# The output tensor as accumulator: b3 and the output tiles of both output layers added by accumulating DMAs

## The reference

```python
xn = layernorm(x)                     # x: 8192 x 2048
a  = (xn @ W_in[:4096].T) @ conv_w.T  # 8192 x 4096
z  = silu(xn @ W_in[4096:].T)
g  = a * D * z
h1 = relu(xn @ W1.T + b1)             # 8192 x 4096
h2 = relu(h1 @ W2.T + b2)
out = x + g @ W_out.T + h2 @ W3.T + b3   # 8192 x 2048
```

## Time and profile before

| | us |
|---|---|
| median of three runs | 1817.83 (1816.61 to 2179.19) |
| the profiled execution | 1814.43 |
| its span on the slowest core (0) | 1812.9 |
| spans of the eight cores | 1805.3 to 1812.9 |
| PE busy | 1764.7 (97%) |
| DVE busy | 900.0 (50%) |
| ACT busy | 229.6 (13%) |
| POOL busy | 243.4 (13%) |
| DMA moved | 296.34 MB, mean 163 GB/s |

### The profile page before, as it was taken

One profiled execution on the slowest core, in us unless ns is written; L12 is line 12 of the kernel. 1 busy time (PEld: TensorE's weight loads), 2 busy tenths in 40 slices (PEclk: granted clock), 3 DMA queues, 4 the chain that ended last, 5 costly groups with the idle time before them and its releaser, 6 DMA issues.

```text
span 1812.9 us, 24809 instructions; the slowest of 8 cores (1805.3 to 1812.9 us)
## 1 busy us (share of the span) xinstructions
PE 1764.7 (97%) x9984; PEld 978.1 (54%) x9984; DVE 900.0 (50%) x1130; ACT 229.6 (13%) x355; POOL 243.4 (13%) x270
## 2 busy tenths in 40 slices
PE   2999999999999999999999999999999999999998
PEld 2444444444444444444444444444444888888887
DVE  6744444444444585444444753333334754466443
ACT  4111122222222200000000011111111000000000
POOL 6222230000000000000000000000000122222221
PEclk9899999999999999999999999999999999999999
DMA  9576764444438543334444822333336765885532
GB/s 290 153 217 216 229 209 124 124 137 140 126 121 276 158 150 117 122 122 133 140 140 155 286 86 96 109 116 116 117 116 207 247 197 175 263 272 186 163 117 71
DMA packets 58016, 296.34 MB, mean 163 GB/s; under 512 B 7600, under 2 KB 7600, under 8 KB 40368
## 3 DMA queue, kind: packets, MB, share of 16 engines
q1 hardware_dynamic: 29376, 167.79, 31.4%
q0 software_dynamic: 28240, 126.89, 19.8%
q10 hardware_dynamic: 288, 0.08, 0.0%
HBM read 227.62 MB, written 67.11 MB: 163 GB/s over the span
## 4 chain that ended last, share of the span: by engine, by line
PE 93%; DMA 3%; DVE 2%; issue 1%; ACT 1%; POOL 0%; DVEq 0%; SPq 0%; ACTq 0%; POOLq 0%
PE ps L293 73%; PE ps L850 19%; DMA sF<-H1S 1%; DMA PS<-sM 1%; DMA sM<-XB 1%; DVE sF L240 1%; DVE sW L240 1%; DMA sF<-X 1%; DVE sST L313 1%; ACT sF L390 0%; PE ps L369 0%; ACT sM L352 0%; DVE sM L335 0%; DVE sM L912 0%; ACT sST L322 0%
## 5 line engine op out<-in xcount | busy, mean ns | idle before, releaser
L293 PE MATMUL ps<-sF,sW 128*128 128x512 bf16 (+1 forms) x6272 | 1357.3, 379 | 4.0 <-DVE sW L240 2.1
L293 PEld LDWEIGHTS ps<-sF,sW 128*128 128x128 f16 x6272 | 613.7, 98 | 746.2 <-issue 9.1
L240 DVE TENSOR_TENSOR sW<-sW 128x1024 f16<-128x1024 f16 (+1 forms) x480 | 446.1, 960 | 168.1 <-DMA sW<-W 127.1
L850 PE MATMUL ps<-sW,sF 128*128 128x256 f16 x3584 | 393.7, 273 | 3.5 <-DVE sW L240 2.0
L850 PEld LDWEIGHTS ps<-sW,sF 128*128 128x128 bf16 x3584 | 351.2, 98 | 46.0 <-issue 4.4
L542 DVE TENSOR_TENSOR sM<-ps,sM 128x512 f32<-128x512 f32 x80 | 55.3, 691 | 331.1 <-ACT sM L537 331.1
L598 DVE TENSOR_TENSOR sM<-ps,sM 128x512 f32<-128x512 f32 (+1 forms) x160 | 109.8, 687 | 119.6 <-PE ps L293 119.6
L537 ACT ACTIVATE sM<-ps 128x512 f32<-128x512 f32 x80 | 47.8, 597 | 606.1 <-PE ps L293 606.1
L240 DVE TENSOR_TENSOR sF<-sF 128x2048 bf16<-128x2048 bf16 (+2 forms) x92 | 101.9, 1169 | 2.9 <-DMA sF<-H1S 2.0
L579 ACT ACTIVATE sM<-sM,sCN 128x512 bf16<-128x512 f32 x64 | 46.0, 721 | 242.3 <-DVE sM L598 242.3
L547 DVE TENSOR_TENSOR sM<-ps,sM 128x512 f32<-128x512 f32 x80 | 54.8, 685 | 22.6 <-PE ps L293 22.6
(11 more groups left out here) (39 smaller groups left out, 347.6 us busy)
## 6 DMA issues: line engine op xcount, KB each, us to landing
sW<-W SPq DMA_DIRECT2D x48, 1024.0 KB, 8.7
sW<-WC SPq DMA_DIRECT2D x32, 1024.0 KB, 7.5
sW<-WX SPq DMA_DIRECT2D x32, 512.0 KB, 6.9
sW<-WZ SPq DMA_DIRECT2D x32, 512.0 KB, 6.6
sW<-W SPq DMA_DIRECT2D x32, 512.0 KB, 6.5
sW<-WO SPq DMA_DIRECT2D x16, 1024.0 KB, 7.9
X1S<-sM POOLq DMA_DIRECT2D x16, 512.0 KB, 7.4
sF<-X POOLq DMA_DIRECT2D x8, 1024.0 KB, 9.8
```

Of the source, the lines that this page charges most:

```text
L240: return line.do(lambda e: e.tensor_tensor(out, a, b, ALU.subtract if sub else ALU.add), c)
L293: return e.matmul(ps[bank][:], sW[:, c0 + k * 128:c0 + (k + 1) * 128], rhs[:, k * TH:(k + 1) * TH], start=st0, stop=last, skip_group_check ...
L850: return e.matmul(ps[bank][:, lo:lo + CW], lhs[:, k * TH + tp * 128:k * TH + (tp + 1) * 128], w[:, k * CW:(k + 1) * CW], start=start, stop ...
```

## The change

- XB and PS are gone. `x_copy(j)` copies 128 rows of X to OUT, from DRAM to DRAM, at the place of `xb_load(j)`; `b3_add(j)`, at the place of `xb_add(j)`, adds BB3 to these rows of OUT by an accumulating DMA, after the copy landed. POOL computes nothing there.
- `r_load` is gone. `o_close` writes the bare result to the ring: for products 3 and 4 a copy on ACT, for 6 and 7 one addition on DVE (bank plus E).
- `r_store(n)` adds the ring's tile to OUT by an accumulating DMA, in both output layers. An item of the second layer waits for the store of the same tile in the first (`n - 32`).
- The ring has 8 buffers, one per item of a chunk; `ring_free` waits for the store of item n - 8, on ACT or DVE, ahead of the close. The first eight wait for the last three stores of H2S.

```diff
+NRING = 8
...
 TM = [
-    dict(w="WO", src="GS", res="XB", dst="PS"),
-    dict(w="W3", src="H2S", res="PS", dst="OUT"),
+    dict(w="WO", src="GS"),
+    dict(w="W3", src="H2S"),
 ]
...
         def ring(i):
-            return sM[:, 2048 + i * 512:2048 + (i + 1) * 512]
+            return sM[:, 1024 + i * 512:1024 + (i + 1) * 512]
...
-        def xb_load(j):
...
-        def xb_add(j):
...
+        def x_copy(j):
+            rows = slice(j * 128, (j + 1) * 128)
+            tk_bs[("l", j)] = pool.do(lambda e: e.dma_start(dram["OUT"][rows, :], dram["X"][rows, :]),
+                                      c_bx[j % 2], 16)
+
+        def b3_add(j):
+            rows = slice(j * 128, (j + 1) * 128)
+            pool.need(tk_bs[("l", j)])
+            tk_bs[j] = pool.do(lambda e: e.dma_start(dram["OUT"][rows, :], dram["BB3"][:], accum_op=ALU.add,
+                                                        max_dma_last_dim=4096),
+                               c_bs[j % 2], 16)
...
-                bg = [tk_bs[6], tk_bs[7], tk_ba.get(7)]
+                bg = [tk_norm[j] for j in range(6)]
...
             if g < 16 and g % 2 == 1:
-                xb_load(g // 2)
+                x_copy(g // 2)
             if 1 < g <= 16 and g % 2 == 0:
-                xb_add(g // 2 - 1)
+                b3_add(g // 2 - 1)
...
-        def r_load(n):
...
         def r_store(n):
+
             si, c, m, u = items[n]
-            i = n % 6
-            pool.need(tk_ro[n])
-            dst = place(TM[si]["dst"], si, c, m, u)
-            tk_rst[n] = pool.do(lambda e: e.dma_start(dst, ring(i).rearrange("p (b i) -> p b i", b=2)), c_rs[i], 16)
+            i = n % NRING
+            pool.need(tk_ro[n], tk_rst.get(n - 32))
+            if n == 0:
+                pool.need(tk_bs[6], tk_bs[7])
+            dst = place("OUT", si, c, m, u)
+            tk_rst[n] = pool.do(lambda e: e.dma_start(dst, ring(i).rearrange("p (b i) -> p b i", b=2),
+                                                      accum_op=ALU.add), c_rs[i], 16)
...
+        def ring_free(line, n):
+
+            if n < NRING:
+                line.need(*e_start, *[tk_store[x] for x in (L, L - 1, L - 2)])
+            else:
+                line.need(tk_rst[n - NRING])
+
         def o_close(n):
             si, c, m, u = items[n]
-            r = ring(n % 6)
+            r = ring(n % NRING)
             bank = ps[OB["A" if m in (3, 6) else "B"][u]][:]
             if m in (3, 4):
-                dve.need(tk_pe[("o", si, c, m, u)], tk_rl[n])
-                tk_ro[n] = dve.do(lambda e: e.tensor_tensor(r, bank, r, ALU.add), c_dve)
+                act.need(tk_pe[("o", si, c, m, u)])
+                ring_free(act, n)
+                tk_ro[n] = act.do(lambda e: e.activation(r, bank, AF.Copy, bias=0.0, scale=1.0), c_act)
                 return
...
+            dve.need(tk_pe[("o", si, c, m, u)], ot[("e", u)])
+            ring_free(dve, n)
+            tk_ro[n] = dve.do(lambda e: e.tensor_tensor(r, bank, e_buf(u), ALU.add), c_dve)
+            ot[({6: "c22", 7: "c11"}[m], u)] = tk_ro[n]
```

More of the change, by code:

```diff
@@ L100, in build_program @@
         dram[name] = nc.dram_tensor(name, [128, 4 * 16 * TH], BF16, kind="Internal")
-    for name in ("XB", "PS"):
-        dram[name] = nc.dram_tensor(name, [TC, HID], F32, kind="Internal")
     sp, pool, pe, dve, act = Line(), Line(), Line(), Line(), Line()
@@ L122, in build_program @@
     c_bs = [ctr(f"bs{i}") for i in range(2)]
-    c_b3 = ctr("b3")
-    c_rl = [ctr(f"rl{i}") for i in range(6)]
-    c_rs = [ctr(f"rs{i}") for i in range(6)]
+    c_rs = [ctr(f"rs{i}") for i in range(NRING)]
     with ExitStack() as ctx:
@@ L500, in build_program @@
         tk_bs = {}
-        tk_ba = {}
-        def xb_load(j):
[L504 to L512, removed]
-        def xb_add(j):
[L515 to L520, removed]
+        def x_copy(j):
[8 more added lines that the diff above has]
+                               c_bs[j % 2], 16)
         tk_s2, tk_d, tk_e, tk_c22, tk_c11 = {}, {}, {}, {}, {}
@@ L859, in build_program @@
         items = [(si, c, m, u) for si in range(2) for c in range(NCH) for m in (3, 4, 6, 7) for u in range(2)]
-        tk_rl, tk_ro, tk_rst = {}, {}, {}
-        ps_stored = []
+        tk_ro, tk_rst = {}, {}
         def place(name, si, c, m, u):
@@ L867, in place, with r_store @@
             return dram[name][r0:r0 + 256, c0:c0 + CW].rearrange("(b p) i -> p b i", b=2)
-        def r_load(n):
+        def r_store(n):
             si, c, m, u = items[n]
-            i = n % 6
[L872 to L877, removed]
+            i = n % NRING
+            pool.need(tk_ro[n], tk_rst.get(n - 32))
             if n == 0:
                 pool.need(tk_bs[6], tk_bs[7])
[L880 to L885, removed]
-            pool.need(tk_ro[n])
-            dst = place(TM[si]["dst"], si, c, m, u)
-            tk_rst[n] = pool.do(lambda e: e.dma_start(dst, ring(i).rearrange("p (b i) -> p b i", b=2)), c_rs[i], 16)
+            dst = place("OUT", si, c, m, u)
+            tk_rst[n] = pool.do(lambda e: e.dma_start(dst, ring(i).rearrange("p (b i) -> p b i", b=2),
+                                                      accum_op=ALU.add), c_rs[i], 16)
         def o_snap(si, c, u):
@@ L950, in build_program @@
         o_sum(0, 0, 1, sum_slots[0][2])
-        PREF = 4
         def finish_pairs():
@@ L979, in close_items @@
                 r_store(n)
-                if n + PREF < len(items):
-                    r_load(n + PREF)
         for x, (si, c) in enumerate(chunks):
@@ L986, in build_program @@
             phase_oa(x)
-            if x == 0:
-                for n in range(PREF):
-                    r_load(n)
             for u in range(2):
@@ L1044, in build_program @@
                 new_forms(6, 4, [tk_pe[("o", si, c, 7, 1)]])
-        for n in range(len(items) - 6, len(items)):
+        for n in range(len(items) - NRING, len(items)):
             pool.need(tk_rst[n])
```

12 lines of the change are left out of this document (removed).

## The result

The change made the kernel slower by 0.3%: in the first comparison the median went from 1816.60 us to 1821.59, and the ratio is 1.0031 (95% interval 1.0021 to 1.0041). On another chip it was 1.0026 (1.0014 to 1.0038). The forecast was 2.8 us less. It is 5 us more. All ratios leave out the executions, found with every kernel, in which the cores of one die or of both had a lower granted clock and the time was longer by some per cent.

What follows compares the result with a forecast made beforehand. PE, busy for 97% of the span, was taken to bound the kernel. Residual loads -4.1 us and the end +1.3 gave -2.8, other terms nothing: 1815 us against a median of 1817.83, range 1808 to 1830.

Steps and rivals of the forecast that it cites:

- x_copy and b3_add: First stage: copy 3.4 to 6.8 us, add likewise, a round's DMA 17 to 24 of 24.0 us; costs nothing.
- a share of 0.85: First stage: DMA engines' busy share after the change, taking 3.4 us for the copy and 6.8 for the add.
- POOL mostly doesn't wait: First stage: b3_add waits for the copy's landing, put at 9.8 us by the X load, with 12 us between issues.
- Rival C: First stage alone short of DMA if b3_add takes over 16.6 us per MB; 1820 to 1838 us, chance 0.07.
- the residual loads: Output layers: 64 loads and DVE's waits on them go; core 0 gains 5.2 us, the slowest core 4.1.
- The stalls of 0.98, 0.45 and 2.02 us: PE's waits on core 0: 0.98 in the output layers' first chunk, 0.45 and 2.02 at their switch; all go.
- the switch: Between the two output layers: 2.47 us of stall and 1.7 us of lower clock (0.91) on core 0 go.
- The end: Behind the last matmul: -0.9 us for the close, +2.2 for the last accumulating store, sum +1.3 us.
- the output layers hide the rest: Output layers: accumulating stores, 5.2 us each, are hidden in all but the last; the ring gives 48 us.
- rival B: Output layers: accumulating stores don't overlap, 8 chunks cost 81 us; 1899 us, slower by 4.5%, chance 0.09.

Runs made afterwards that it cites:

- lag: The changed kernel with each b3_add issued one round (two pairs, 24 us) later, three pairs behind its copy; ratio 0.9999 to the kernel before.
- oldbg: The changed kernel's output layers, with X + b3 loaded, added and stored by POOL as before; ratio 0.9976, on another chip 0.9973, to the kernel before.
- oldout: The changed kernel's copies and b3 adds, with the output layers of before (residual loads, plain stores, ring of 6); ratio 1.0033 to the kernel before.
- plain2: oldbg with plain stores in place of the 64 accumulating ones, sums left out of the output; ratio 0.9960 to the kernel before.
- noacc3: The changed kernel with b3_add as a plain copy of BB3 over the rows, x left out; ratio 0.9969 to the kernel before.

## Why the prediction was wrong

**The step that failed** is "x_copy and b3_add", by its terms "the copy from DRAM to DRAM costs 3.4 (one pass) to 6.8 us" and "the accumulating one likewise 3.4 to 6.8", with "it fits at both ends" as its conclusion. The copy measured 4.8 us, inside. The add measured 9.4 us (10 by the averages), outside: a load and a store of SBUF one after the other were no upper end for it. With the 9.6 us of WX and X1S (0.40 of 24) a round needs 23.8 of its 24.0 us. I had called a share of 0.85, and it was 0.91 to 1.03. The rule of the Trainium skill that I weighed ("Collectives: The Full Stack", section "The bandwidth ceiling: the fold count and why AG ≠ RS ≠ AR", on why an adding transfer runs at about half the rate) gives an estimate of 2 x 4.8 = 9.6 us if it is applied to the copy's measured price. The runs agree with it within what the prices are good for (9.4 to 4.8 is 2.0, and 10 to 4.2 is 2.4), though they show the ratio and not its cause; I had applied it to the price of an SBUF transfer.

**The second fault of that step** was "POOL mostly doesn't wait", argued from a landing of 9.8 us in a queue that had room. In the full queue a copy lands in 25.2 us. And what stands behind POOL's wait I had named (the X1S store, three staging buffers) but given one sentence, and no price. By lag it is about half of the loss.

**Rival C was the right rival with the wrong point.** It let the first layer run short of DMA, but measured it by the weight loads, which are 50 us ahead: 16.6 us for each MB added. Those loads did slow to 15.0 us, and no engine waited for them. The limit was the queue's own round, with X1S stores in it that have two pairs of slack: 24.0 - 9.6 - 4.8 = 9.6 us, and the add costs 9.4. Its expected sign, PE waiting for WX, was never seen; PE waited for ACT, and ACT for a store.

**Right: the residual loads.** The stalls of 0.98, 0.45 and 2.02 us went from core 0 (0.3 us is left on core 6), and the granted clock behind the switch is 1.00, where the earlier trace rows have 0.91. DVE is 42 us less busy (44 forecast), POOL 48 (37 forecast). I put the slowest core's gain at 4.1 us; with 1.3 us for the end the half by itself came to -2.8. oldbg measured 4.4 and 4.9 us (0.9976 of 1813.7, 0.9973 of 1815.3).

**The end had a term that I missed.** I had +1.3 us, -0.9 for the close and +2.2 for the last accumulating store. The close gave 2.11 - 1.29 = 0.82. The last store lands 4.1 to 4.9 us after its issue and not 2.5, so 2.2 more was a good price. But behind that landing the span ends 1.4 us sooner than before. oldout, with the output layers of before, still has the longer tail (2.7 to 2.9 us), and plain2, with those of the change and plain stores, the shorter one (1.2 to 1.4), so it comes with the new output layers and not with the adding; what in them does it stays open. Together the way from the last store's issue to the end grew by 0.2 us on core 0 (5.57 for 5.34) and by 1.0 on core 1 (1806.2 - 1799.83 = 6.37, before 5.33), and the end moved by -0.6 to +0.2 us and not by +1.3. This is part of why oldbg gained more than 2.8 us. The median landing of 6.0 us is that of stores beside others.

**Right: the output layers hide the rest.** Landings of 6.0 us at the median and 20.9 at most are under the 48 us of the ring, and rival B (no overlap, 81 us) didn't come. POOL's issue went from 0.71 to 1.20 us, a cost that I had not named; it is hidden. (In rival B a chunk's excess is 58.4 - 48.4 = 10.0 us and not 10.1, which changes nothing.)

**Luck, and what a measurement can tell.** The median lies inside my range by the luck of its width. The sign was wrong. I had also taken it that this kernel's measurements can't tell less than 2%; the intervals here are 0.1% wide to either side, and a difference of 0.3% is clear.

## What to carry to other kernels

Price a new kind of transfer for the queue and the round in which it stands, not by the average share of the DMA engines: a round that is full gets later each time, until something waits. Ask of each DMA that waits on its issuing engine which stores are issued behind it, and who needs their buffers back. A background task goes where a round has room and no layer's blocks are about to be loaded, its second half well behind its first.

## What the runs showed of the hardware

- An accumulating DMA of 1 MB from DRAM to DRAM cost 9.4 us of all sixteen engines, a copy of it 4.8 us (each good to about 1 us), and a load or store of SBUF about 3.4. The bytes that the page counts don't rise with it, but the share does: the changed kernel and noacc3 both have 218.19 MB read and 75.50 MB written, and shares of 1.01 and 0.87 on core 1 in the window from 90 to 135 us.
- In the full queue mostly one core of each pair falls behind and the other doesn't: adds 29.1 us apart on core 0, and 26.1 on core 1 (84.9 to 267.7 us). Which of the two it is changes between executions, and a smaller gap of 5 to 7 us was there before the change.
- An accumulating store of 256 KB from SBUF lands in 4.1 us at best and 6.0 at the median, a plain one in 2.8 at the median, and takes POOL 1.20 us to issue and not 0.71.
